# Projection of q, k and v in an attention layer: one float32 product in place of three float32r products, conversions of two blocks at once, stores with longer runs

## The chip, the cores and the metric

One Trainium2 chip, one core of it. The metric is the device time of one launch in microseconds (us). Shorter is better.

## The reference

A transformer layer on x of shape (4, 2048, 256) in float32: normalization, sliding-window attention with 16 heads of 16, and a feed-forward part with ternary weights. The change concerns the first lines, in which q, k and v are made for all 8192 tokens.

```python
xn = _layernorm(x)
q = (xn @ Wq.T).reshape(Bb, Tt, H, HD).transpose(0, 2, 1, 3)
k = (xn @ Wk.T).reshape(Bb, Tt, H, HD).transpose(0, 2, 1, 3)
v = (xn @ Wv.T).reshape(Bb, Tt, H, HD).transpose(0, 2, 1, 3)
logits = jnp.einsum('bhqd,bhkd->bhqk', q, k) * SCALE      # |i-j| <= 128, or token 0
out = jnp.einsum('bhqk,bhkd->bhqd', softmax(where(attend, logits, -inf)), v)
x = x + out.transpose(0, 2, 1, 3).reshape(Bb, Tt, D) @ Wo.T
x = x + bitlinear(relu(bitlinear(_layernorm(x), w_fc) + gate * low_rank)**2, w_proj)
```

## The kernel before, in words

Three stages follow each other: `stage_project` (q, k, v, and the row of token 0), `stage_attend`, `stage_feed`. Only the first is rewritten; in the second only the loads of v follow a new layout in DRAM.

**The loop.** The 8192 tokens are 16 groups of 512 (4 tiles of 128). `step(body, i)` runs a software pipeline on every engine: in iteration i the group i is loaded, i-1 gets its statistics (`n`, LN), i-2 its factor (`f`, LF), i-3 is scaled and transposed (`t`, LT), and i-4 is multiplied (`q`, LP). Order within an engine is the order of the code; between engines there are semaphores only.

**TensorE (PE).** One iteration has four products u = 0..3 (q block 0, q block 1, k block 0, k block 1; each 128 of the 256 outputs by 512 tokens, one PSUM bank each, `qk_bank[u]`), then four products of v (128 tokens by 272 columns, in two banks by turns). `turn()`, the 8 transposes of the next group (L528), stands between u = 2 and u = 3 and waits for `norm.s_scaled`, which ScalarE raises after the last of four scalings (L233). The operands are split: `xt_hi` is the float32r rounding of the transposed x, `xt_lo` the rest, and the weights likewise. `three_pass` makes hi x hi, hi x lo and lo x hi, for two halves of the contraction: six matmuls (L253, L254, L255) for each u and for each v tile. The trace prints float32r operands of matmuls as f32; the names `_hi` and `_lo` tell them apart.

**ScalarE (ACT).** It scales x into `xn` (L233), rounds each finished bank to bf16 (`high`, L608), rounds the rest (`mid`, L613), makes `xt_hi` (L655), and moves v to SBUF (`v`, L618).

**VectorE (DVE).** `rest_of` (L729, L733) subtracts the high part, L761 makes `xt_lo`; the rest is statistics (L142, L202), the factor (`factor_begin`, `factor_end`), and `weights.dve_part`, preparation of the ternary weights.

**GpSimd (POOL).** L448 makes the low bf16 part of q and k, and L459 fills the columns between key blocks (`s_gap`).

**SyncE (SP)** issues every DMA. An iteration: load of x, stores of three parts of q as they are done, three stores of k after `s_gap`, one store of v. After the last group it issues the loads of unit 1, waits for all stores and for the row of token 0 (`s_rv`), stores the row, and only then ends its stage. After the last product the row takes a chain of its own: L573, L576, L581 (64 float32 products of 272 columns, on four column groups of the array), L585 (one float32 product of 272 columns).

Of the kernel before, what the change touches and what calls it, by code (L numbers as in the profile page):

```python
# [31 lines left out]
P = 128  # L32
# [12 lines left out]
VROW = H * VW  # L45
EPS = 1e-5
# [226 lines left out]
def stage_project(nc, x, attn_w, q_dram, k_dram, va_dram, o_dram, weights, sh):  # L273
# [6 lines left out]
    NB, QR, VS = T // P, 32, VROW + VW  # L280
    with ExitStack() as ctx:  # L281
# [10 lines left out]
        xt_hi = sb("xt_hi", [P, 2, KT, GT], F32R)  # L292
        w_in = sb("w_in", [P, 3, KT, D])
        wt_hi = sb("wt_hi", [P, 2, KT, D], F32R)
        wt_lo = sb("wt_lo", [P, 2, KT, D], F32R)
        wv_hi = sb("wv_hi", [P, B, KT, D + H], F32R)
        wv_lo = sb("wv_lo", [P, B, KT, D + H], F32R)
# [9 lines left out]
        xt_lo = sb("xt_lo", [P, 2, KT, GT], F32R)  # L307
# [3 lines left out]
        q_parts = sb("q_parts", [P, 2, KT, PARTS, GT], BF16)  # L311
        k_parts = sb("k_parts", [P, 2, KT, PARTS, KGT], BF16)
        key0, one = sb("key0", [P, KT, PARTS], BF16), sb("one", [P, PARTS], BF16)
# [8 lines left out]
        banks = [ctx.enter_context(nc.psum_tensor(f"p_bank{i}", [P, GT], F32)) for i in range(8)]  # L322
# [10 lines left out]
        s_wt, s_whi, s_wlo, s_wv = sem("w_turned"), sem("w_hi"), sem("w_lo"), sem("wv_copies")  # L333
        s_x0, s_x0v, s_x0sd, s_x0pe = sem("x0_in"), sem("x0_vector"), sem("x0_sd"), sem("x0_tensor")
        s_chi, s_clo = sem("c_hi"), sem("c_lo")
        s_x = [sem(f"x_in{i}") for i in range(4)]
        s_t, s_hi, s_lo = sem("turned"), sem("xt_hi"), sem("xt_lo")
# [16 lines left out]
        def part_of(q, u, part):  # L354
            place = PLACE[u // KT][part]
            if u < KT:
                return q_parts[:, q.par, u, place, :].rearrange("p (n e) -> p n e", e=P)
            return k_parts[:, q.par, u - KT, place, :].rearrange("p (n e) -> p n e", e=KPITCH)[:, :, 1:KPITCH]

        def blocks(bank):  # L360
            return bank[:].rearrange("p (n e) -> p n e", e=P)
# [4 lines left out]
        def _(sp):  # L366
# [15 lines left out]
            def body(at):  # L382
# [8 lines left out]
                if q := at(LP):  # L391
                    rows = q_dram[bass.ds(q.g, 1)].rearrange("a i d s h m t -> (a i d) s (h m t)")
                    for part, done in ((HIGH, s_high), (MID, s_mid), (LOW, s_low)):
                        sp.wait_ge(done, q.g * 4 + KT)
                        sp.dma_start(rows[:, PLACE[0][part]], q_parts[:, q.par, :, PLACE[0][part]]
                                     ).then_inc(s_qout[q.par], DMA)
                    rows = k_dram[bass.ds(q.g, 1)].rearrange("a i d s h m t -> (a i d) s (h m t)")
                    sp.wait_ge(s_gap, q.g * KT + KT)
                    for place in range(PARTS):
                        sp.dma_start(rows[:, place], k_parts[:, q.par, :, place]).then_inc(s_kout[q.par], DMA)  # L400
# [16 lines left out]
        def _(pool):  # L417
# [4 lines left out]
            pool.memset(va[:, :, 0:VROW].rearrange("p n (h e) -> p n h e", e=VW)[:, :, :, HD:VW], 1.0  # L422
# [14 lines left out]
            def wv_copies(b):  # L437

                pool.wait_ge(s_whi, 4)
                pool.tensor_copy(wv_hi[:, b, :, 0:D], wv_hi[:, 0, :, 0:D]).then_inc(s_wv, 1)  # L440
                pool.wait_ge(s_wlo, 3)
                pool.tensor_copy(wv_lo[:, b, :, 0:D], wv_lo[:, 0, :, 0:D]).then_inc(s_wv, 1)

            def body(at):
                if q := at(LP):
                    for u in range(2 * KT):
                        pool.wait_ge(s_mid, q.g * 4 + u + 1)
                        pool.tensor_tensor(part_of(q, u, LOW), rest[:, u, :].rearrange("p (n e) -> p n e", e=P),  # L448
                                           part_of(q, u, MID), ALU.subtract).then_inc(s_low, 1)
                        if u < KT:  # L450
                            continue
                        m = u - KT
                        keys = k_parts[:, q.par, m].rearrange("p s (n e) -> p s n e", e=KPITCH)
                        pool.wait_ge(s_low, q.g * 4 + u + 1)
                        if q.of_batch == 0:
                            wait(pool, s_gap, (q.g - 1) * KT + m + 1)
                            pool.tensor_tensor(key0[:, m, :], keys[:, :, 0, 1], one[:], ALU.mult).then_inc(s_key0, 1)
                            pool.wait_ge(s_key0, q.batch * KT + m + 1)
                        pool.tensor_tensor(keys[:, :, :, 0], key0[:, m, :].unsqueeze(2).broadcast_to([P, PARTS, TB]),  # L459
                                           one[:].unsqueeze(2).broadcast_to([P, PARTS, TB]), ALU.mult  # L460
                                           ).then_inc(s_gap, 1)
# [13 lines left out]
        def _(pe):  # L475
# [13 lines left out]
            def first_queries():  # L489
                pe.wait_ge(s_x0v, 10)  # L490
                pe.wait_ge(s_whi, 2)
# [25 lines left out]
            def wv(tile, q):  # L517
                return [tile[:, bass.ds(q.batch, 1), k, :].rearrange("p a n -> p (a n)") for k in range(KT)]

            def body(at):  # L520
                def turn():

                    if q := at(LT):
                        pe.wait_ge(norm.s_scaled, q.g + 1)
                        for k in range(KT):
                            wait(pe, s_lo, (q.g - 1) * KT + k + 1)
# [1605 lines left out]
```

## Time and profile before

| | us |
|---|---|
| median of three runs (1153.77, 1153.78, 1153.89) | 1153.78 |
| span of the profiled execution | 1152.4 |
| projection products, first to last | 13.2 to 166.7 |
| row of token 0, end of the first stage | 166.7 to 183 |
| attention and feed-forward | 183 to 1152.4 |

The page gives the span of the profiled execution, from first to last instruction, and no other time of it; the span is 1.4 us below the median of the timed runs. Starts in the timeline are us from the beginning of the span. A matmul's row starts when it starts to stream; its end is modelled and includes the pipeline behind it, so rows overlap, and what one costs its successor is the distance of the starts.

### The profile page before, as it was taken

The numbers are of one execution on the slowest core, as the hardware profiler recorded it, in microseconds if no ns is written. First come the engines' busy times: TensorE is split into PE (matmuls) and PEld (weight loads), VectorE is DVE, ScalarE is ACT, GpSimd is POOL, SyncE is SP. The second block draws the span as 40 slices with busy tenths as digits, with TensorE's granted clock in tenths as the row PEclk, the third lists the DMA queues.
The fourth block names the chain that finished last, engine by engine and source line by source line (L and its number), as shares of the span: only waits on it lengthen the run. The fifth ranks groups of instructions, "written<-read, shape, count | busy, mean of one in ns | idle before, by whom it ended". The sixth has DMA issues, their size and how long they took to land.

```text
span 1152.4 us, 26576 instructions
## 1 busy us (share of the span) xinstructions
PE 1126.9 (98%) x9115; PEld 785.0 (68%) x9115; DVE 979.5 (85%) x3169; ACT 843.4 (73%) x1513; POOL 706.8 (61%) x935
## 2 busy tenths in 40 slices
PE   9999997999999999999999999999999999999998
PEld 8888884455555555555555455558888988898887
DVE  7889857899889998899889999867888888888885
ACT  7989983788888888888788888875465546554654
POOL 3665565677778777887778877773344334433443
PEclk9999998999999999999999999999999999999999
DMA  6999897555555555545565554240232113211201
GB/s 199 295 296 281 257 266 168 114 131 118 137 133 122 132 125 136 132 115 137 126 138 130 114 138 108 68 139 29 74 102 64 56 55 102 64 55 56 74 20 37
DMA packets 158166, 145.24 MB, mean 126 GB/s; under 512 B 21564, under 2 KB 157776, under 8 KB 158032
## 3 DMA queue, kind: packets, MB, share of 16 engines
q1 hardware_dynamic: 158032, 143.54, 48.8%
q8 instruction: 73, 1.20, 0.5%
q14 instruction: 61, 0.50, 0.2%
HBM read 91.74 MB, written 50.95 MB: 124 GB/s over the span
## 4 chain that ended last, share of the span: by engine, by line
PE 73%; DVE 7%; issue 2%; ACT 1%; POOL 1%; DVEq 0%; POOLq 0%; ACTq 0%
PE e_psum L1549 15%; PE e_psum L1503 15%; PE e_psum L1527 14%; PE e_psum L1844 6%; PE e_psum L1846 5%; PE e_psum L1267 3%; PE e_psum L1825 3%; PE e_psum L1824 3%; DVE n_stats L142 2%; DVE f_x L1958 2%; PE e_psum L1829 1%; PE e_psum L255 1%; PE e_psum L254 1%; PE e_psum L253 1%; PE e_psum L1793 1%
## 5 line engine op out<-in xcount | busy, mean ns | idle before, releaser
L1665 DVE CUSTOM_DVE_ANT_0 a_masked<-e_psum,band 128x387 f32<-128x387 f32 (+1 forms) x1024 | 493.3, 534 | 58.8 <-PE e_psum L1503 55.8
L1622 ACT ACTIVATE a_weights<-e_psum 128x1024 f32<-128x1024 f32 (+1 forms) x512 | 398.0, 806 | 87.2 <-PE e_psum L1527 82.2
L1401 POOL TENSOR_SCALAR_AFFINE_SELECT a_weights<-a_weights 128x1024 f32<-128x1024 f32 x256 | 276.2, 1091 | 59.9 <-ACT a_weights L1622 58.7
L1503 PE MATMUL e_psum<-e_k,e_q 96*128 96x387 bf16 (+1 forms) x1024 | 281.4, 327 | 3.0 <-PEq L281 1.4
L1888 POOL TENSOR_TENSOR f_square<-f_relu 128x512 f32<-128x512 f32 x128 | 146.1, 1142 | 209.6 <-ACT f_relu L1877 198.6
L1527 PE MATMUL e_psum<-e_q,e_k 128*128 128x384 bf16 (+2 forms) x1408 | 255.6, 279 | 1.5 <-ACT a_weights L1622 1.1
L1549 PE MATMUL e_psum<-a_weights,a_v 128*17 128x384 f32 (+2 forms) x2816 | 195.8, 392 | 1.0 <-POOL a_weights L1401 1.0
L1527 PEld LDWEIGHTS e_psum<-e_q,e_k 128*128 128x128 bf16 x1408 | 129.0, 98 | 95.6 <-issue 39.5
L1503 PEld LDWEIGHTS e_psum<-e_k,e_q 96*128 96x128 bf16 x1024 | 100.4, 98 | 99.2 <-DVE a_max L1665 44.8
L1844 PE MATMUL e_psum<-w_w_t,f_square_hi 128*128 128x256 f32 x512 | 129.4, 287 | 5.6 <-DVE f_square_lo L1934 5.6
L1846 PE MATMUL e_psum<-w_w_t,f_square_lo 128*128 128x256 f32 x512 | 126.8, 282 | 0.0
L1877 ACT ACTIVATE f_relu<-e_psum,w_mag 128x512 f32<-128x512 f32 x128 | 87.2, 681 | 52.6 <-PE e_psum L1829 52.6
L1934 DVE TENSOR_TENSOR f_square_lo<-f_square,f_square_hi 128x512 fp32r<-128x512 f32 x128 | 98.5, 789 | 24.2 <-POOL f_square L1888 24.2
L1549 PEld LDWEIGHTS e_psum<-a_weights,a_v 128*17 128x17 f32 x2816 | 61.7, 96 | 67.5 <-issue 53.6
L1844 PEld LDWEIGHTS e_psum<-w_w_t,f_square_hi 128*128 128x128 f32 x512 | 96.7, 189 | 15.1 <-DVE f_square_lo L1934 12.1
L1824 PE MATMUL e_psum<-f_xt_hi,w_w_t 128*128 128x512 f32 x256 | 102.8, 402 | 1.1 <-ACT f_relu L1877 1.1
L1825 PE MATMUL e_psum<-f_xt_lo,w_w_t 128*128 128x512 f32 x256 | 101.3, 396 | 0.0
L1846 PEld LDWEIGHTS e_psum<-w_w_t,f_square_lo 128*128 128x128 f32 x512 | 97.0, 189 | 2.8
L1880 ACT ACTIVATE f_square_hi<-f_relu 128x512 fp32r<-128x512 f32 x128 | 81.0, 633 | 4.1
L448 POOL TENSOR_TENSOR p_q_parts<-p_rest,p_q_parts 128x512 bf16<-128x512 f32 x32 | 38.3, 1196 | 70.0 <-ACT p_q_parts L613 69.9
L1665 DVE DVE_READ_ACCUMULATOR2_ANT a_max<- 128x1 f32 x1024 | 78.9, 77 | 0.0
L1870 ACT ACTIVATE f_z<-e_psum 128x512 fp32r<-128x512 f32 x16 | 9.6, 597 | 90.1 <-PE e_psum L1816 90.1
(219 smaller groups left out, 2059.0 us busy)
## 6 DMA issues: line engine op xcount, KB each, us to landing
k_parts<-p_k_parts SPq DMA_DIRECT2D x48, 258.0 KB, 4.6
e_k<-k_parts SPq DMA_DIRECT2D x64, 193.5 KB, 3.6
e_k<-k_parts SPq DMA_DIRECT2D x192, 64.5 KB, 3.3
q_parts<-p_q_parts SPq DMA_DIRECT2D x48, 256.0 KB, 5.1
e_q<-q_parts SPq DMA_DIRECT2D x64, 192.0 KB, 3.7
e_q<-q_parts SPq DMA_DIRECT2D x192, 64.0 KB, 3.3
v_ones<-p_va SPq DMA_DIRECT2D x16, 544.0 KB, 5.9
p_x<-in_x SPq DMA_DIRECT2D x16, 512.0 KB, 6.3
```

Source lines behind the costliest of these rows:

```text
L1401: pool.affine_select(out=blocks, in_=blocks, compare_op=ALU.is_ge, fill=0.0, base=0, pattern=[[0, NQ // 2 * HEAD_COLS // P // CUT_STEP], [ ...
L1503: pe.matmul(sh.tile_bank(ux, j)[:, lo:hi], qw[ux.q][0:SLOT_ROWS, h, t * P:t * P + P], kt[ux.hq][0:SLOT_ROWS, h, start + lo:start + hi], st ...
L1527: ins = pe.matmul(score[third // 2][:, c0:c0 + m * P], kt[us.hq][:, h, k0:k0 + P], qw[us.q][:, h, qb * P:(qb + m) * P], start=True, stop=True)
L1549: ins = pe.matmul(sum_bank[32 * j:32 * j + VW, qb * P:(qb + m) * P], vw[:, up.gpar, kb + 1, h * VW:h * VW + VW], pe_w[:, up.upar, c0:c0 + ...
L1622: act.activation(pe_w[:, us.upar, lo:hi], score[c % 2][:], ACT.Exp).then_inc(s_exp, 1)
L1665: dve.tensor_tensor_reduce(out=masked[:, ux.upar, h, t:t + hi - lo], in0=bank[:, lo:hi], in1=band[:, lo:hi], scale=1.0, scalar=NEG, op0=AL ...
L1824: pe.matmul(self.h_bank[j % 2][:], lhs, self.sh.xt_hi[:, q.par, k, :], start=(k == 0), stop=False)
L1825: pe.matmul(self.h_bank[j % 2][:], lhs, self.sh.xt_lo[:, q.par, k, :], start=False, stop=False)
L1844: pe.matmul(y, sh.r2_hi[:, j % 4, part], self.w.w2_t[:, j, :], start=(j == 0 and t == 0), stop=False, skip_group_check=True)
L1846: ins = pe.matmul(y, sh.r2_lo[:, j % 4, part], self.w.w2_t[:, j, :], start=False, stop=(j == MH - 1), skip_group_check=True)
L1888: pool.tensor_tensor(sh.r2[:, j % 4, :], sh.r[:, j % 4, :], sh.r[:, j % 4, :], ALU.mult).then_inc(self.s_sq, 1)
L1934: dve.tensor_tensor(sh.r2_lo[:, j % 4, :], sh.r2[:, j % 4, :], sh.r2_hi[:, j % 4, :].bitcast(F32), ALU.subtract).then_inc(self.s_r2lo, 1)
```

## The change

- `three_pass` goes from q, k and v. Each u and each v tile is two float32 matmuls (the two halves of the contraction), accumulated.
- `xt_lo`, `wt_lo`, `wv_lo` and what made them go. The transposed x (`xt`) is float32: half 0 is copied by ScalarE, half 1 by VectorE, one copy of 512 columns each.
- `high`, `rest`, `mid` and `low` work on two blocks (1024 columns, two PSUM banks) at a time: once for q, once for k. `high(Q)` stands where `high(0)` stood, and waits for u = 0 and u = 1. The scalings of tiles 2 and 3, which stood behind `high(0)` and `high(1)`, both stand behind `high(Q)`.
- `q_parts` and `k_parts` in SBUF have the part outside the block, so that a store moves 2048 or 2064 bytes per partition in one run where it moved two runs of half that. `va_dram` is [128, 64, 289] instead of [8192, 272]: a store or load moves the whole of a partition in one run. `vw` in the second stage is 289 wide. SBUF stays filled with unused pieces (`hole0` to `hole2`) in place of the tensors that went.

```diff
                 if q:
-                    pe.wait_ge(s_lo, q.g * KT + KT)
-                    xh = [xt_hi[:, q.par, k, :] for k in range(KT)]
-                    xl = [xt_lo[:, q.par, k, :] for k in range(KT)]
+                    for k in range(KT):
+                        pe.wait_ge(s_xt[k], q.g + 1)
                 for u in range(2 * KT):
                     if u == KT + 1:
                         turn()
...
-                        wait(pe, s_rest, (q.g - 1) * 4 + u + 1)
-                        three_pass(pe, qk_bank[u][:], [wt_hi[:, w, k, m:m + P] for k in range(KT)],
-                                   [wt_lo[:, w, k, m:m + P] for k in range(KT)], xh, xl).then_inc(s_qk, 1)
+                        if u % KT == 0:
+                            wait(pe, s_rest, (q.g - 1) * 2 + w + 1)
+                        for k in range(KT):
+                            ins = pe.matmul(qk_bank[u][:], wt[:, w, k, m:m + P], xt[:, q.par, k, :],
+                                            start=(k == 0), stop=(k == KT - 1))
+                        ins.then_inc(s_qk, 1)
...
-                        three_pass(pe, v_bank[t % 2][:, 0:D + H], [a[:, cut] for a in xh], [a[:, cut] for a in xl],
-                                   wv(wv_hi, q), wv(wv_lo, q)).then_inc(s_v, 1)
+                        for k in range(KT):
+                            ins = pe.matmul(v_bank[t % 2][:, 0:D + H], xt[:, q.par, k, t * P:(t + 1) * P],
+                                            wv[:, q.batch, k, :], start=(k == 0), stop=(k == KT - 1))
+                        ins.then_inc(s_v, 1)
...
+                def high(w):
+                    act.wait_ge(s_qk, q.g * 4 + w * KT + KT)
+                    wait(act, (s_qout, s_kout)[w][q.par], q.half * DMA * STORES)
+                    act.activation(part_of(q, w, HIGH), products(w), ACT.Copy,
+                                   scale=QSCALE if w == Q else 1.0).then_inc(s_high, 1)
...
                 if q:
-                    high(0)
+                    high(Q)
...
                     norm.scale_act(act, xb[:, t.ring], xn[:, t.par], t, (2,))
-                if q:
-                    high(1)
-                if t and t.g != 1:
                     norm.scale_act(act, xb[:, t.ring], xn[:, t.par], t, (3,))
-                if q:
-                    high(2)
...
-                    sp.dma_start(va_dram[bass.ds(q.g * GT, GT), :].rearrange("(t p) n -> p t n", p=P),
-                                 va[:, bass.ds(q.g * TB, TB), 0:VROW]).then_inc(s_vstored, DMA)
+                    sp.dma_start(va_dram[:, q.g * TB:(q.g + 1) * TB, :], va[:, q.g * TB:(q.g + 1) * TB, :]
+                                 ).then_inc(s_vstored, DMA)
```

On ScalarE, one iteration of the steady part of the projection reads as follows before, from the scaling of tiles 0 and 1 to the first copy of v (`p_bank` are the PSUM banks, `p_rest` the rests):

```order
L233 ACTIVATE p_xn<-p_x,n_shift,n_rstd 128x256 x2
L608 ACTIVATE p_q_parts<-p_bank 128x512
L207 ACTIVATE n_stddev<-n_meanvar,n_eps 128x4
L233 ACTIVATE p_xn<-p_x,n_shift,n_rstd 128x256
L608 ACTIVATE p_q_parts<-p_bank 128x512
L233 ACTIVATE p_xn<-p_x,n_shift,n_rstd 128x256
L608 ACTIVATE p_k_parts<-p_bank 128x4x128
L655 ACTIVATE p_xt_hi<-p_bank 128x512 x2
L613 ACTIVATE p_q_parts<-p_rest 128x512
L608 ACTIVATE p_k_parts<-p_bank 128x4x128
L618 ACTIVATE p_va<-p_bank 128x17x16
```

The same iteration on ScalarE in the changed kernel, to its end (`p_psum` are the PSUM banks as one tensor):

```order
L234 ACTIVATE p_xn<-p_x,n_shift,n_rstd 128x256 x2
L612 ACTIVATE p_q_parts<-p_psum 128x1024
L208 ACTIVATE n_stddev<-n_meanvar,n_eps 128x4
L234 ACTIVATE p_xn<-p_x,n_shift,n_rstd 128x256 x2
L651 ACTIVATE p_xt<-p_psum 128x512
L612 ACTIVATE p_k_parts<-p_psum 128x8x128
L621 ACTIVATE p_va<-p_psum 128x17x16 x2
L617 ACTIVATE p_q_parts<-p_rest 128x1024
L621 ACTIVATE p_va<-p_psum 128x17x16 x2
L617 ACTIVATE p_k_parts<-p_rest 128x8x128
```

The last two scalings stood apart, each behind one block of q; now both stand behind the conversion of the two blocks together.

On TensorE, the changed kernel's iteration, from u = 0 to the first product of the next one (each matmul is one row here, whatever it becomes on the chip; before there were 18, 8, 6, 24 in the same places):

```order
L550 MATMUL p_psum<-p_xt,p_wt 128x512 x6
L530 MATMUL p_psum<-p_ident,p_xn 128x128 x8
L550 MATMUL p_psum<-p_xt,p_wt 128x512 x2
L562 MATMUL p_psum<-p_wv,p_xt 128x272 x8
```

The transposes stay in their place: six products ahead of them, of which only the last two (u = 2) come after what `high(Q)` waits for.

## Rows read from the trace of the kernel before

**Rows 1.** The page: span; engine, busy us, share, instructions.

```profile
span 1152.4 us, 26576 instructions
PE 1126.9 (98%) x9115; PEld 785.0 (68%) x9115; DVE 979.5 (85%) x3169; ACT 843.4 (73%) x1513; POOL 706.8 (61%) x935
```

**Rows 2.** Stretches: us; busy of PE, PEld, DVE, ACT, POOL; granted clock; DMA share; GB/s.

```profile
13.20:166.70 153.50, 152.97 (x896) 133.60 (x897) 127.78 (x331) 137.21 (x298) 86.86 (x111) 1.00 0.93 264
91.39:100.95 9.56, 9.56 (x59) 8.35 (x57) 9.30 (x23) 8.77 (x20) 5.22 (x7) 1.00 0.96 286
```

**Rows 3.** Timeline of PE over one iteration: start, us, engine, line, operation.

```profile
91.39 0.40 PE L253 MATMUL p_bank<-p_xt_hi,p_wt_hi 128*128 128x512 f32 x1
...
94.19 0.40 PE L253 MATMUL p_bank<-p_xt_hi,p_wt_hi 128*128 128x512 f32 x1
...
95.35 0.40 PE L255 MATMUL p_bank<-p_xt_hi,p_wt_lo 128*128 128x512 f32 x1
95.58 1.04 PE L528 MATMUL p_bank<-p_ident,p_xn 128*128 128x128 f32 x8
96.38 0.49 PE L253 MATMUL p_bank<-p_xt_hi,p_wt_hi 128*128 128x512 f32 x1
...
97.87 0.29 PE L253 MATMUL p_bank<-p_wv_hi,p_xt_hi 128*128 128x272 f32 x1
...
100.14 0.35 PE L253 MATMUL p_bank<-p_wv_hi,p_xt_hi 128*128 128x272 f32 x1
...
100.95 0.40 PE L253 MATMUL p_bank<-p_xt_hi,p_wt_hi 128*128 128x512 f32 x1
```

**Rows 4.** Timeline of PE behind the projection: float32 products with four column groups, then one.

```profile
169.95 2.50 PE L487 MATMUL p_bank<-p_ones 128*128 128x128 f32 x20
172.62 7.53 PE L581 MATMUL p_bank<-p_va,p_w 128*16 128x272 f32 x128 [0.16 <-ACT p_w L681]
181.04 0.62 PE L585 MATMUL p_bank<-p_picked,p_seq_of 128*4 128x272 f32 x2 [0.90 <-DVE p_picked L819]
```

**Rows 5.** Line L585: duration ns min/median/max, first and last start.

```profile
L585 PE MATMUL p_bank<-p_picked,p_seq_of x2: 393/393/393, 181.0 to 181.3; 128*4 128x272 f32 x2
```

**Rows 6.** Timeline of ACT around the transposes of the iteration of rows 3.

```profile
93.48 0.29 ACT L207 ACTIVATE n_stddev<-n_meanvar,n_eps 128x4 f32<-128x4 f32 x1
93.67 0.59 ACT L233 ACTIVATE p_xn<-p_x,n_shift,n_rstd 128x256 f32<-128x256 f32 x1
94.38 0.60 ACT L608 ACTIVATE p_q_parts<-p_bank 128x512 bf16<-128x512 f32 x1
94.88 0.59 ACT L233 ACTIVATE p_xn<-p_x,n_shift,n_rstd 128x256 f32<-128x256 f32 x1
```

**Rows 7.** An ACT read of 1024 columns of PSUM, 183 to 290 us; count, busy, mean ns.

```profile
L1622 ACT ACTIVATE a_weights<-e_psum 128x1024 f32<-128x1024 f32 x39 | 39.9, 1024 | 10.7 <-PE e_psum L1527 9.9
```

**Rows 8.** Timeline of PE and PEld ahead of the first product of the projection.

```profile
10.53 0.86 PEld L528 LDWEIGHTS p_bank<-p_ident,p_xn 128*128 128x128 f32 x8 [0.65 <-ACT p_xn L233]
12.28 0.64 PE L480 MATMUL p_bank<-p_ident,p_w_in 128*128 128x128 f32 x4
13.21 0.50 PE L253 MATMUL p_bank<-p_xt_hi,p_wt_hi 128*128 128x512 f32 x1 [0.29 <-DVE p_xt_lo L761]
```

**Rows 9.** Groups within 13.2 to 166.7 us; count, busy us, mean ns, idle before.

```profile
L448 POOL TENSOR_TENSOR p_q_parts<-p_rest,p_q_parts 128x512 bf16<-128x512 f32 x32 | 38.3, 1196 | 70.0 <-ACT p_q_parts L613 69.9
L729 DVE SCALAR_TENSOR_TENSOR p_rest<-p_bank,p_q_parts 128x512 f32<-128x512 f32 x32 | 22.0, 688 | 15.3 <-ACT p_q_parts L608 15.0
L613 ACT ACTIVATE p_k_parts<-p_rest 128x512 bf16<-128x512 f32 x32 | 20.3, 635 | 1.2 <-DVE p_rest L733 1.2
L618 ACT ACTIVATE p_va<-p_bank 128x272 f32<-128x272 f32 x63 | 25.1, 399 | 2.6 <-PE p_bank L255 2.1
```

**Rows 10.** Timelines of SP, POOL and DVE in the tail of the first stage.

```profile
170.07 2.28 SPq L400 DMA_DIRECT2D k_parts<-p_k_parts  x3
180.24 1.53 SPq L1230 DMA_DIRECT2D e_q<-q_parts  x3
182.21 0.26 SPq L414 DMA_DIRECT2D attention<-row  x1
169.57 0.25 POOL L459 TENSOR_TENSOR p_k_parts<-p_key,p_one 128x12 bf16<-128x12 bf16 x1
181.70 0.41 DVE L823 COPY row<-p_bank 4x256 f32<-4x256 f32 x1 [0.71 <-PE p_bank L585]
```

More of the change, by code:

```diff
@@ L45 @@
 VROW = H * VW
+VS = VROW + VW
 EPS = 1e-5
@@ L321, in stage_project @@
         row, s_row = sh.row, sh.s_row0
-        banks = [ctx.enter_context(nc.psum_tensor(f"p_bank{i}", [P, GT], F32)) for i in range(8)]
+        psum = ctx.enter_context(nc.psum_tensor("p_psum", [P, 8, GT], F32))
+        banks = [psum[:, i, :] for i in range(8)]
         t_bank, qk_bank, v_bank = banks[0:2], banks[2:6], banks[6:8]
@@ L352, in stage_project, with part_of, products, rest_of @@
         LN, LF, LT, LP = 1, 2, 3, 4
[L354 to L361, printed above, removed]
+        Q, K = 0, 1
+        def part_of(q, w, part):
+            place = PLACE[w][part]
+            if w == Q:
+                return q_parts[:, q.par, place].rearrange("p m (n e) -> p (m n) e", e=P)
+            return k_parts[:, q.par, place].rearrange("p m (n e) -> p (m n) e", e=KPITCH)[:, :, 1:KPITCH]
+        def products(w):
+            return psum[:, 2 + KT * w:2 + KT * w + KT, :].rearrange("p m (n e) -> p (m n) e", e=P)
+        def rest_of(w):
+            return rest[:, KT * w:KT * w + KT, :].rearrange("p m (n e) -> p (m n) e", e=P)
         block = ctx.enter_context(nc.Block())
@@ L437, in wv_copies @@
             def wv_copies(b):
[L439 to L442, printed above, removed]
+                pool.wait_ge(s_wc, 4)
+                pool.tensor_copy(wv[:, b, :, 0:D], wv[:, 0, :, 0:D]).then_inc(s_wv, 1)
             def body(at):
                 if q := at(LP):
[L446 to L461, printed above, removed]
@@ new lines, in body @@
+                    for w in (Q, K):
+                        pool.wait_ge(s_mid, q.g * 2 + w + 1)
+                        pool.tensor_tensor(part_of(q, w, LOW), rest_of(w), part_of(q, w, MID), ALU.subtract
+                                           ).then_inc(s_low, 1)
+                    keys = k_parts[:, q.par].rearrange("p s m (n e) -> p s m n e", e=KPITCH)
+                    pool.wait_ge(s_low, q.g * 2 + 2)
+                    if q.of_batch == 0:
+                        wait(pool, s_gap, q.g)
+                        pool.tensor_tensor(key0[:], keys[:, :, :, 0, 1], one[:].unsqueeze(2).broadcast_to([P, PARTS, KT]),
+                                           ALU.mult).then_inc(s_key0, 1)
+                        pool.wait_ge(s_key0, q.batch + 1)
@@ L462, in body @@
+                    for m in range(KT):
+                        ins = pool.tensor_tensor(keys[:, :, m, :, 0], key0[:, :, m].unsqueeze(2).broadcast_to([P, PARTS, TB]),
+                                                 one[:].unsqueeze(2).broadcast_to([P, PARTS, TB]), ALU.mult)
+                    ins.then_inc(s_gap, 1)
                     if 1 <= q.g < B:
```

164 lines of the change are left out of this document (63 added, 101 removed).

## The prediction

> **What bounds the kernel now.** I read the page first: TensorE is busy for 98% of the span, VectorE for 85% [rows 1]. Such an average says nothing of one stage, so I cut the projection out, and one iteration of it. In the 153.5 us from the first to the last product TensorE is idle for 0.5 us; in the iteration from 91.39 to 100.95 it is never idle, while VectorE has 9.30 of 9.56 us busy, ScalarE 8.77, GpSimd 5.22, and the DMA engines 0.96 [rows 2]. TensorE sets the pace of this stage, the others follow with little room. The clock granted is 1.00, the full 2.4 GHz [rows 2]. What the edit does to TensorE therefore shows in full, and what it does for the other engines and the stores shows only if TensorE has to wait for them.
>
> **The distance of starts on TensorE, before.** u = 0 to 2 are 18 float32r matmuls of 512 columns in 95.58 - 91.39 = 4.19 us, 0.2328 each. The transposes take 96.38 - 95.58 = 0.80 us, and u = 3, six matmuls, 97.87 - 96.38 = 1.49 us, which is 0.09 over six times 0.2328, for the weights that are loaded in the open behind the transposes. So transposes cost 0.89. v: the first 18 matmuls take 100.14 - 97.87 = 2.27 us, 0.126 each; all 24 take 3.08, with a short hitch in front of the last tile [rows 3]. Sum: 24 x 0.2328 + 0.89 + 3.08 = 9.56, the iteration.
>
> **What a float32 product costs.** The rows have float32 products too, with real operands: L585 is one matmul in the code and two rows on the chip, of 393 ns each, and the two together last 0.62 us; so the second starts 0.62 - 0.393 = 0.227 us behind the first [rows 4, 5]. One float32 product of 272 columns thus takes two instructions of 0.227 us, 0.454 in all, where three float32r ones take 3 x 0.126 = 0.378. L581 says the same in bulk: 128 instructions for 64 products, 7.53 us, with four column groups at work at a time; (7.53 - 0.39)/127 x 4 = 0.225 [rows 4]. 0.227 us for 272 columns is 0.834 ns a column, twice what one pass at 2.4 GHz needs; two instructions make four passes.
>
> L581 and L585 load narrow weights. The rows with 128 x 128 float32 weights are L487: 20 instructions of 128 columns in 2.50 us, (2.50 - 0.27)/19 = 0.117 [rows 4], against 0.107 by columns; so up to 0.010 an instruction is to be added, and I take half. For 512 columns no float32 row exists: 512 x 0.834 = 0.427 is the floor, twice 0.2328 = 0.466 the ceiling, if a float32 pass streams no faster than a float32r one. I take 0.433, near the floor, since at 272 columns the float32 instruction (0.227) is clearly below twice the float32r one (0.252). For v I take 0.232, between 0.227 and 0.252.
>
> - q and k: 16 instructions x 0.433 = 6.93 us, where 24 x 0.2328 = 5.59 were: +1.34.
> - v: 16 x 0.232 = 3.71, where 3.08 were: +0.63.
> - Together +1.97 an iteration, 16 iterations: **+31.5 us.**
>
> The Trainium skill ("FP8 and Floating Point Precision", TensorE Precision Notes) says that a true float32 product takes four passes through the array; L585 agrees with its 0.454 us, four passes of 0.113 us. The rule alone would price a pass by the float32r rows; that result is rival B below.
>
> **A wait that the new order makes.** `turn()` waits for the last scaling. Now this is queued on ScalarE behind `high(Q)`, which waits for u = 1. Let T be the time when u = 1 has streamed. Before, its last matmul ended streaming at 94.19 and its conversion began at 94.38: 0.19 [rows 3, 6]. The conversion of 1024 columns out of PSUM: L1622 has 1.02 us [rows 7], and ScalarE starts the next instruction 0.1 before the end of the last (0.60 long, next after 0.50) [rows 6], so 0.92. The root of the variance 93.48 to 93.67: 0.19. The scaling of tile 2: 0.50, of tile 3 to its end: 0.59 [rows 6]. From there to the first transpose 0.06 (the end of a scaling at about 10.48, its weight load at 10.53 [rows 8]). T + 0.19 + 0.92 + 0.19 + 0.50 + 0.59 + 0.06 = T + 2.45. TensorE is there after u = 2: T + 4 x 0.433 = T + 1.73. It waits 0.72 us. Before, the same chain had only half a conversion behind u = 1 and was over at 95.47, just before 95.58 [rows 3, 6], so the wait is new. It occurs where both a group to multiply and a group to transpose are there, without the first (group 1 is scaled early): 14 times, **+10.1 us**. Queued behind TensorE's wait are u = 3 and v, all of the rest.
>
> **Does another wait appear?** With an iteration of 6.93 + 0.89 + 0.72 + 3.71 = 12.25 us, I followed each engine through it, S being the end of u = 3. ScalarE: `high(K)` begins at S + 0.19, the first copy of v ends at S + 1.5 (0.40 long [rows 9]); the third v tile needs it at S + 1.86. The next scalings start at about S + 5.2 and end at S + 6.3, ahead of the next T at S + 7.2. VectorE loses one of the two 512-column passes behind the transposes and keeps about 9 us of 12.25; its passes over 1024 columns are below twice 0.69 us [rows 9] and each bank has over 3 us before it is written again. GpSimd's are below twice 1.2 us [rows 9] and make 5.2 of 12.25. The stores have half the runs and a longer iteration. All of these edits, the fused conversions (a saving of about 0.1 us each), the missing `xt_lo`, the longer runs, I cost at nothing: behind TensorE's 12.25 us. If TensorE were not the bound, they would be worth something, see the third rival. The loads of v in the attention stage are prefetched; nothing waits for them in the rows, so nothing is gained.
>
> **Ends.** The first product waited 0.29 us for `xt_lo`, which is gone [rows 8]: **-0.3**. In the tail, SP was busy with its issues until 180.24 + 1.53 = 181.77, and the row was ready at 182.11 [rows 10], so only 0.3 us lay between. SP's chain begins when the last key columns are filled: 169.57 + 0.25 = 169.82, 3.10 us after the last product (166.72). Now ScalarE's `mid(K)` (0.96) stands behind the last copy of v, and GpSimd's `low(K)` of two blocks (2.3) and two fills behind that: mid(K) ends 1.5 us after the last product, low(Q) keeps GpSimd until 2.0, low(K) until 4.3, the fills until 4.9. That is 1.8 later, less the 0.3 to 0.4 of room and less what shorter stores save in issue, which I can't read: between 0 and 1.5, I take **+1.1** (the row's own chain moves with the products).
>
> **Sum** against the profiled execution: 1152.4 + 31.5 + 10.1 - 0.3 + 1.1 = 1194.8 us; the runs shown lie 1.4 above their span, which gives 1196.2 us.
>
> **The rivals.**
> - *B, slower still: a float32 pass streams at the float32r distance.* For it: float32r at 512 columns takes 0.2328, not 0.213, and I have no float32 row of that width with wide weights. Against it: L585. Then 16 x 0.466 = 7.45 and 16 x 0.252 = 4.03: +2.81 an iteration, 45.0; the wait shrinks to 2.45 - 1.86 = 0.59, 8.3; with the ends 54.1: 1207.9 us. By the rule of four passes from the page named above and the float32r row, this would be the time. Chance 0.12.
> - *C, the products at their floor and no wait at the transposes* (if ScalarE converts two banks faster, or the release of the bank is earlier than I think). 16 x 0.427 + 16 x 0.227 = 10.46, against 8.67: +1.79, 28.6, with the ends 29.4: 1183.2 us. With half of the wait it is some 1188. Chance 0.14.
> - *D, faster: one float32 instruction costs no more than one float32r instruction*, so that two take the place of three. This needs 0.2328 at 512 columns, and decides for a gain as soon as an instruction is below 0.33 or so. Then TensorE needs 3.72 + 0.89 + 2.02 = 6.6, and waits 2.45 - 0.93 = 1.5 at the transposes: 8.15; VectorE and ScalarE with some 8.4 us would be the bound: 16 x (8.4 - 9.56) = -18.6: 1136 us. For it: only that the distance of L487 may be set by its weight load. Against it: L585, where nothing but streaming lies between the two starts, and L581. Chance 0.03.
> - *E, the edit moves TensorE little in either direction*, because something else than the columns sets the distances: within 0.2% of before, chance 0.01.
> - The forecast, with waits a little longer or shorter: 1188 to 1204 us, chance 0.70.
>
> **How the numbers follow.** The likeliest is 1196.2. Below 1183 I leave D, E and part of C, 0.08; above 1209 what lies beyond B (a chain that comes late on VectorE or SP as well), 0.08. Two thousandths of the time, 2.3 us, is about what a measurement of this kernel can tell from no change. Faster by more than that: D alone, 0.03. No change: E, 0.01. Slower: the rest, 0.96.
>
> **What the profile after would show.** Right: L550 with twice its count of instructions (256 rows), starts 0.43 apart; L562 0.23 apart; an iteration of 12.2 to 12.3 us; PE idle in front of L530 with ScalarE's L234 as releaser, some 0.7 us, 14 times; VectorE and ScalarE with 3 us idle in each iteration; the attention stage as long as before. Wrong: starts of L550 at 0.47 (B), at 0.23 (D), no idle time before L530 (C), or PE waiting for `p_rest`, `p_xt` or `p_va`.

## The result and the profile after

The changed kernel takes 1196.26 us (median of three runs, 1194.24 to 1196.48), the kernel before 1153.78; the ratio is 1.036, 95% interval 1.034 to 1.038. Slower, as forecast, and close to the 1196.2 of the prediction. Whether its terms are right is another matter, and one of them isn't.

The page of the changed kernel, its head:

```profile
span 1194.2 us, 25872 instructions
PE 1160.0 (97%) x8859; PEld 761.7 (64%) x8859; DVE 973.0 (81%) x3115; ACT 831.8 (70%) x1433; POOL 696.2 (58%) x896
PEclk9999999889999999999999999999999999999999
```

Three stretches of it, columns as in [rows 2]: the products of the projection, the row of token 0, the rest.

```profile
12.77:206.07 193.30, 185.63 (x642) 109.55 (x641) 121.36 (x278) 125.55 (x218) 75.12 (x73) 1.00 0.67 219
206.07:224.89 18.82, 14.83 (x170) 9.68 (x169) 12.17 (x28) 5.14 (x7) 11.08 (x14) 0.91 0.67 168
224.89:1194.20 969.31, 948.38 (x7976) 632.01 (x7976) 831.97 (x2773) 694.31 (x1195) 605.06 (x793) 0.99 0.41 101
```

The same stretches of the kernel before:

```profile
13.21:166.72 153.51, 152.99 (x897) 133.62 (x898) 127.77 (x331) 137.22 (x298) 86.88 (x111) 1.00 0.93 264
166.72:183.07 16.35, 13.28 (x171) 8.17 (x170) 10.83 (x28) 4.71 (x7) 9.66 (x15) 1.00 1.04 263
183.07:1152.40 969.33, 949.39 (x7976) 632.93 (x7976) 832.06 (x2773) 694.15 (x1195) 605.37 (x793) 0.99 0.41 100
```

The first product starts 0.44 us earlier, the products take 39.8 us more, the row 2.5 more, and attention with feed-forward is the same to 0.02 in these two profiles (over all thirteen profiles of this document it lies between 968.0 and 970.0 us, so a difference of a microsecond there says nothing). Together 41.8 us, the difference of the spans. The medians differ by 42.5: the time outside the span is 2.1 us here (1196.26 with a span of 1194.2) and was 1.4. TensorE is idle for 7.7 of its 193.3 us, where it was 0.5 (all of that 0.5 in one iteration, which took 10.47 us where the others took 9.5 to 9.6: the scaling came late there, by 0.52 us, as the row below shows); VectorE is busy for 63% of the stretch where it was 83%, the DMA engines 0.67 for 0.93.

```profile
76.47 1.09 PE L528 MATMUL p_bank<-p_ident,p_xn 128*128 128x128 f32 x8 [0.52 <-ACT p_xn L233]
```

One iteration on TensorE, the answer to [rows 3]. The rows are merged where nothing lies between the instructions:

```profile
98.22 5.31 PE L550 MATMUL p_psum<-p_xt,p_wt 128*128 128x512 f32 x12
104.09 1.09 PE L530 MATMUL p_psum<-p_ident,p_xn 128*128 128x128 f32 x8 [0.56 <-ACT p_xn L234]
105.02 1.88 PE L550 MATMUL p_psum<-p_xt,p_wt 128*128 128x512 f32 x4
106.74 3.83 PE L562 MATMUL p_psum<-p_wv,p_xt 128*128 128x272 f32 x16
110.41 5.31 PE L550 MATMUL p_psum<-p_xt,p_wt 128*128 128x512 f32 x12
```

Six matmuls in the code are 12 instructions, as L585 foretold. One lasts 0.592 (median of L550), so their distance is (5.31 - 0.592)/11 = 0.429 us; u = 3 takes (106.74 - 105.02)/4 = 0.43; v takes (110.41 - 106.74)/16 = 0.229. The iteration is 12.19 us. In front of the transposes the profile names ScalarE's scaling. From the end of streaming (98.22 + 12 x 0.429 = 103.37) to 104.09 it is 0.72 us; the 0.56 of the row is less because the modelled end of the last product reaches past its streaming.

ScalarE in this stretch, the answer to [rows 6]:

```profile
101.85 1.02 ACT L612 ACTIVATE p_q_parts<-p_psum 128x1024 bf16<-128x1024 f32 x1 [1.11 <-PE p_psum L550]
102.77 0.29 ACT L208 ACTIVATE n_stddev<-n_meanvar,n_eps 128x4 f32<-128x4 f32 x1
102.96 1.08 ACT L234 ACTIVATE p_xn<-p_x,n_shift,n_rstd 128x256 f32<-128x256 f32 x2
104.84 0.60 ACT L651 ACTIVATE p_xt<-p_psum 128x512 f32<-128x512 f32 x1 [0.81 <-PE p_psum L530]
```

This is the chain of the prediction: ScalarE had waited 1.11 us for u = 1, then converts 1024 columns, takes the root, scales two tiles until 104.04, and the transposes start at 104.09. While it does so TensorE comes to rest (a rest is, here and below, time in which it streams nothing).

The tail is what follows the last product: a chain of small steps in turn on TensorE and VectorE makes the row of token 0. `m_diag`, a diagonal of maxima that VectorE writes, is one link of it. First what TensorE does there:

```profile
207.64 0.27 PE L578 MATMUL p_psum<-p_ident,p_m_tok 128*64 128x128 f32 x1
210.12 0.43 PE L581 MATMUL p_psum<-p_m_diag,p_ones 64*128 64x64 f32 x2 [1.77 <-DVE p_m_diag L776]
210.48 4.10 PE L492 MATMUL p_psum<-p_ones 128*128 128x128 f32 x20
```

Here are two losses the forecast didn't have: 1.77 us idle for `m_diag`, where it was 0.60, and 4.10 us for the 20 products that took 2.50 [rows 4]. VectorE and GpSimd at that place:

```profile
207.96 2.06 POOL L454 TENSOR_TENSOR p_k_parts<-p_rest,p_k_parts 128x1024 bf16<-128x1024 f32 x1
208.27 1.80 DVE L776 TENSOR_SCALAR p_m_diag<-p_ident,p_m_neg 64x64 f32<-64x64 f32 x1
```

GpSimd's instruction ends at 210.02, VectorE's at 210.07. In the kernel before the two end at 169.49 and 169.54:

```profile
168.37 1.12 POOL L448 TENSOR_TENSOR p_k_parts<-p_rest,p_k_parts 128x512 bf16<-128x512 f32 x1
168.91 0.63 DVE L806 TENSOR_SCALAR p_m_diag<-p_ident,p_m_neg 64x64 f32<-64x64 f32 x1
```

And the granted clock around it, in the changed kernel:

```profile
209.00:210.10 1.10, 0.00 (x0) 0.00 (x0) 1.07 (x1) 1.08 (x2) 1.02 (x2) 1.00 0.62 238
210.10:212.00 1.90, 1.88 (x11) 1.81 (x12) 1.41 (x6) 0.28 (x1) 1.69 (x6) 0.76 0.15 58
212.00:214.50 2.50, 2.50 (x13) 2.29 (x11) 2.36 (x9) 1.06 (x1) 2.50 (x3) 0.50 1.03 395
214.50:218.00 3.50, 3.50 (x65) 1.79 (x68) 3.08 (x8) 0.00 (x0) 2.90 (x4) 1.00 0.99 221
```

Behind the idle time the clock is at 0.50, the 1.2 GHz level, and at 1.00 again from 214.5. It doesn't fall in the rest itself: it is 1.00 until 211.0, when TensorE has been at work again for 0.9 us, and falls in the half microsecond after:

```profile
211.00:211.50 0.50, 0.50 (x5) 0.50 (x5) 0.50 (x3) 0.00 (x0) 0.50 (x2) 0.60 0.00 0
```

Before, it was 1.00 all through 166.7 to 183.

### The profile page after: what moved, and what is told of

Same layout as the page of the kernel before. It is cut to its first block, busy times and chain, and to the rows that moved or that the text cites. A ratio compares the mean times of both kernels' runs of the same rounds, so it can differ in the third digit from the quotient of the medians.

```text
span 1194.2 us, 25872 instructions
## 1 busy us (share of the span) xinstructions
PE 1160.0 (97%) x8859; PEld 761.7 (64%) x8859; DVE 973.0 (81%) x3115; ACT 831.8 (70%) x1433; POOL 696.2 (58%) x896
## 3 DMA queue, kind: packets, MB, share of 16 engines
q8 instruction: 71, 1.16, 0.4%
## 4 chain that ended last, share of the span: by engine, by line
PE 70%; DVE 7%; issue 2%; ACT 1%; POOL 0%; DVEq 0%; POOLq 0%; ACTq 0%
PE e_psum L1518 15%; PE e_psum L1472 14%; PE e_psum L1496 14%; PE e_psum L1813 5%; PE e_psum L1815 5%; PE e_psum L1237 3%; PE e_psum L1794 3%; PE e_psum L1793 3%; DVE n_stats L143 2%; DVE f_x L1927 2%; PE e_psum L1798 1%; PE e_psum L256 1%; PE e_psum L255 1%; PE e_psum L254 1%; PE e_psum L1762 1%
## 5 line engine op out<-in xcount | busy, mean ns | idle before, releaser
L1634 DVE CUSTOM_DVE_ANT_0 a_masked<-e_psum,band 128x387 f32<-128x387 f32 (+1 forms) x1024 | 493.4, 534 | 58.6 <-PE e_psum L1472 55.6
L550 PE MATMUL p_psum<-p_xt,p_wt 128*128 128x512 f32 x256 | 115.2, 593 | 0.0
L454 POOL TENSOR_TENSOR p_q_parts<-p_rest,p_q_parts 128x1024 bf16<-128x1024 f32 x16 | 34.2, 2136 | 122.9 <-ACT p_q_parts L617 122.9
```

Of the source, the lines that this page charges most:

```text
L550: ins = pe.matmul(qk_bank[u][:], wt[:, w, k, m:m + P], xt[:, q.par, k, :], start=(k == 0), stop=(k == KT - 1))
L1634: dve.tensor_tensor_reduce(out=masked[:, ux.upar, h, t:t + hi - lo], in0=bank[:, lo:hi], in1=band[:, lo:hi], scale=1.0, scalar=NEG, op0=AL ...
```

## The experiments

Each time stands beside the kernel before on the same chip, whose median was 1153.13 in the first four, 1153.42 in the second four, 1152.51 for the ninth and tenth and 1152.69 for the last. Single runs of before spread over 1151.4 to 1155.4, so a difference of 1 us between kernels of different sets is none. Two repairs come up again and again: "the scalings ahead" takes away the wait at the transposes, "the halves" shortens the wait for `m_diag`.

### The products alone (on the kernel before)

```diff
-                        three_pass(pe, qk_bank[u][:], [wt_hi[:, w, k, m:m + P] for k in range(KT)],
-                                   [wt_lo[:, w, k, m:m + P] for k in range(KT)], xh, xl).then_inc(s_qk, 1)
+                        for k in range(KT):
+                            ins = pe.matmul(qk_bank[u][:], wt_hi[:, w, k, m:m + P], xh[k], start=(k == 0), stop=(k == KT - 1))
+                        ins.then_inc(s_qk, 1)
```

and the same for v; the `_hi` tensors are float32.

> The kernel before with the products alone changed: two float32 matmuls instead of six float32r ones; the low parts are still computed, by the same instructions, and nothing reads them. Theory (the columns price the products): q and k 16 x 0.429, v 16 x 0.229, transposes 0.93, so 11.46 us an iteration against 9.56, 16 x 1.90 = 30.4, no wait at the transposes since only half a conversion and one scaling stand behind u = 1 (T + 1.34 against T + 1.72): 1184 us. Rival (the loss comes from the fused conversions and what waits for them, not from the products): under 1165 us.

Measured: 1181.32 us, ratio 1.024 (1.023 to 1.026). The timeline of TensorE, one iteration:

```profile
106.23 5.31 PE L548 MATMUL p_bank<-p_xt_hi,p_wt_hi 128*128 128x512 f32 x12
111.38 1.04 PE L528 MATMUL p_bank<-p_ident,p_xn 128*128 128x128 f32 x8
112.25 1.88 PE L548 MATMUL p_bank<-p_xt_hi,p_wt_hi 128*128 128x512 f32 x4
113.97 3.83 PE L560 MATMUL p_bank<-p_wv_hi,p_xt_hi 128*128 128x272 f32 x16
117.64 2.74 PE L548 MATMUL p_bank<-p_xt_hi,p_wt_hi 128*128 128x512 f32 x6
```

No wait at the transposes, 11.41 us. The products cost 11.41 - 9.56 = 1.85 us an iteration, 29.6 in all. The estimate was 2.7 us high. The kernel before has 0.65 us less in this set; the transposes take 0.87 when they follow products without a rest, not the 0.93 of the changed kernel, which is 0.8 in all; and this kernel's own tail is 0.4 us shorter than before. The remaining 0.8 us is no more than what attention and feed-forward differ by between profiles (968.2 here, 969.3 before). The rival that puts the loss on the conversions falls.

### The other parts, with float32r products

The changed kernel with `three_pass`, the low parts and their subtractions back; fused conversions, long runs and the order on ScalarE stay.

> The changed kernel with the three float32r products back (hi and lo parts made as before), fused conversions and long runs kept. Theory: the wait at the transposes is a matter of the order on ScalarE: T + 2.45 against T + 6 x 0.2328 = T + 1.40, so 1.05 us, 14 times, 14.7 us, and the tail as long as in the changed kernel, +2.5: 1171 us. Rival (fused conversions and long runs pay once the float32 products no longer cover them; VectorE, ScalarE and the DMA engines were near their limit before): 1154 us or less.

Measured: 1171.89 us, ratio 1.016 (1.014 to 1.018). The timeline of TensorE, the transposes of two iterations:

```profile
115.26 1.09 PE L532 MATMUL p_psum<-p_ident,p_xn 128*128 128x128 f32 x8 [0.89 <-ACT p_xn L234]
126.01 1.09 PE L532 MATMUL p_psum<-p_ident,p_xn 128*128 128x128 f32 x8 [0.88 <-ACT p_xn L234]
```

10.75 us from one to the next. The estimate was 1171, and the rival (1154 or less) falls. The wait is larger where the products are shorter, since ScalarE's chain is the same: a price that doesn't come with float32, and that no fused conversion pays back.

### The scalings ahead of the conversion of q

```diff
-                if q:
-                    high(Q)
-                if f and f.g != 1:
-                    norm.root_eps(act, f)
                 if t and t.g != 1:
                     norm.scale_act(act, xb[:, t.ring], xn[:, t.par], t, (2,))
                     norm.scale_act(act, xb[:, t.ring], xn[:, t.par], t, (3,))
+                if q:
+                    high(Q)
+                if f and f.g != 1:
+                    norm.root_eps(act, f)
```

> The changed kernel with the scalings of tiles 2 and 3 ahead of the conversion of the two blocks of q, nothing else. Theory: the 0.72 us in front of the first transpose go, 14 times, 10.1 us, and the conversion starts some 0.3 us late, which nobody waits for: 1186 us. Rival (the wait moves on to the next semaphore, to the rests of q or the copies of x): 1193 us or more.

Measured: 1184.2 us, ratio 1.027 (1.025 to 1.028). The timeline of TensorE, one iteration:

```profile
104.97 5.31 PE L550 MATMUL p_psum<-p_xt,p_wt 128*128 128x512 f32 x12
110.12 1.04 PE L530 MATMUL p_psum<-p_ident,p_xn 128*128 128x128 f32 x8
110.99 1.88 PE L550 MATMUL p_psum<-p_xt,p_wt 128*128 128x512 f32 x4
112.71 3.83 PE L562 MATMUL p_psum<-p_wv,p_xt 128*128 128x272 f32 x16
116.38 4.03 PE L550 MATMUL p_psum<-p_xt,p_wt 128*128 128x512 f32 x9
```

The wait is gone and the iteration 11.41 us, that of the products alone. So a wait costs 12.19 - 11.41 = 0.78 us (0.72 of rest and 0.06 of transposes that start from rest). Thirteen of the 14 cost that and the last 0.59, together 10.7 us: the products, first to last, take 182.6 us here and 193.3 in the changed kernel. The rival falls: the wait doesn't move on. In this profile TensorE was idle in the tail for 1.77 us as well, and yet the 20 products took 2.50, so the tail is 1.4 us shorter; that is most of what the estimate missed, and not a merit of this edit.

### The new layouts alone (on the kernel before)

```diff
-        q_parts = sb("q_parts", [P, 2, KT, PARTS, GT], BF16)
-        k_parts = sb("k_parts", [P, 2, KT, PARTS, KGT], BF16)
+        q_parts = sb("q_parts", [P, 2, PARTS, KT, GT], BF16)
+        k_parts = sb("k_parts", [P, 2, PARTS, KT, KGT], BF16)
...
-    va_dram = nc.dram_tensor("v_ones", [N, VROW], F32, kind="Internal").ap()
+    va_dram = nc.dram_tensor("v_ones", [P, N // P, VS], F32, kind="Internal").ap()
```

> The kernel before with the new layouts alone: parts outside the block in SBUF, v in DRAM as one run per partition; conversions and products as before. Theory: the DMA engines are at 0.96 before but set nothing, so the same within 0.2%: 1153.8 us, DMA share in the projection clearly lower. Rival (the stores hold up x or the key chain): 1150 us or less.

Measured: 1151.76 us (ten runs), ratio 0.9985 (0.9976 to 0.9995): faster by 0.15%, so not quite nothing, though less than the 0.2% named as the bound. The DMA share of the projection is 0.82 for 0.93. In the profile the products take 152.6 us for 153.5, TensorE idle for 0.01 us of it where it was 0.5. The profile before has VectorE waiting for the DMA of x, 2.5 us in two waits, the longer 2.1 us at 64.7 to 66.8 (its view of waits); this one has a single such wait, of 0.3 us. The one iteration of before that took 10.47 us comes from that long wait: VectorE was late with its rests, ScalarE waited 1.16 us for one of them (until 72.39) and was late with the scalings, and TensorE with the transposes at 76.47. Here no iteration is over 9.6. So what the shorter stores took away in the projection is one late load of x: the rival was right in kind, once in 16 groups. That the load was late because of the stores is likely, but one pair of profiles doesn't show it. What is left of the 1.4 us is of the size by which attention and feed-forward differ between profiles (968.0 here, 969.3 before).

### The tail: GpSimd's low parts of the last group in halves

```diff
-                        pool.tensor_tensor(part_of(q, w, LOW), rest_of(w), part_of(q, w, MID), ALU.subtract
-                                           ).then_inc(s_low, 1)
+                        n = KT * TB
+                        for c in ([slice(0, n // 2), slice(n // 2, n)] if q.g == G - 1 else [slice(0, n)]):
+                            ins = pool.tensor_tensor(part_of(q, w, LOW)[:, c], rest_of(w)[:, c],
+                                                     part_of(q, w, MID)[:, c], ALU.subtract)
+                        ins.then_inc(s_low, 1)
```

> The changed kernel with GpSimd's low parts of the last group in two instructions each. Theory: VectorE's step of the row's chain (the diagonal of maxima, 1.80 us where it was 0.63) ends when the GpSimd instruction beside it ends; with halves it ends 1.0 us sooner, TensorE stands idle 0.7 us and not 1.8, and if the idle time is what lets the granted clock fall, another 1.4 us go: 1194 to 1195 us for the wait alone, 1193.8 with the clock. Rival (the step is slow for its own reasons): 1196.3 us, the step still 1.8 us.

Measured: 1193.47 us, ratio 1.035 (1.0335 to 1.0363). The timeline of VectorE:

```profile
208.27 0.99 DVE L779 TENSOR_SCALAR p_m_diag<-p_ident,p_m_neg 64x64 f32<-64x64 f32 x1
```

VectorE's step is 0.81 us shorter and TensorE's rest 0.96 us; the 20 products behind take 2.50 us:

```profile
209.68 2.50 PE L495 MATMUL p_psum<-p_ones 128*128 128x128 f32 x20
```

The profile's span is 1191.2 us, 3.0 below the changed kernel's: 0.8 of the wait, 1.4 of the clock, and 0.9 behind the row, in attention and feed-forward (968.4 for 969.3 us), which no edit touched.

### The tail: products in the gap

```diff
             pe.wait_ge(s_rv, 3)
```

is preceded by `idle_products(total_bank, 6)`, work that nothing reads.

> The changed kernel with six idle products of 128 columns (1.4 us) in TensorE's gap of the row's chain, ahead of the wait for the diagonal. Theory: the wait stays, 1.8 us, but the granted clock of the stretch behind stays at 1.00 and the 20 instructions behind take 2.5 us and not 4.1: 1194.8 us. Rival (the clock falls for another reason): 1196.3 us.

Measured: 1194.85 us, ratio 1.036 (1.034 to 1.037). `m_diag` still takes 1.79 us, and TensorE comes to it at 210.10, as in the changed kernel; but its rest is 0.42 us, and behind it:

```profile
210.46 2.50 PE L492 MATMUL p_psum<-p_ones 128*128 128x128 f32 x20
```

The rows settle it, not the time: the four runs lie in two pairs, 1193.9 and 1194.1, 1195.6 and 1195.8, and those of the changed kernel at 1194.2 and at 1196.3 and 1196.5.

So the wait and the clock are two things, and the second follows the idle time. Over all profiles, that of the kernel before among them: with a rest of at most 1.21 us at this place (nine of them) the 20 products take 2.50 us; with 1.77 to 2.0 us they take 4.05 to 4.13 in three and 2.50 in one, that of the scalings ahead. A long rest lets the clock fall, but not each time.

### Both repairs

The scalings ahead and the halves in the last group.

> The changed kernel with both repairs: scalings ahead of the conversion of q, and the low parts of the last group in halves. Theory: both add up, -10.1 and -1 to -2.5: 1183.7 to 1185 us, all that is left over before being the products. Rival (the two share a cause): 1186 us or more.

Measured: 1182.93 us, ratio 1.026 (1.024 to 1.027). The two add up, and nearly all that is left is the price of the products. It is 1.6 us above the products alone (1181.32), and the runs of the two don't overlap (1182.4 to 1184.2, 1180.6 to 1182.4): TensorE's rest for `m_diag` is still 0.97 us where the products alone have 0.22, and the time outside the span is 2.1 us where it is 1.7.

### Float32r products with the scalings ahead

> Float32r products, fused conversions and long runs, and the scalings ahead of the conversion of q. Theory: no wait at the transposes, TensorE's own sum of 9.5 us an iteration, the tail of the changed kernel (+2.5) less 0.4 to 1: 1155 us, no gain over before, since TensorE bounds both. Rival (the freed time of the others is worth something): under 1150 us.

Measured: 1158.48 us, ratio 1.004 (1.003 to 1.006). The wait at the transposes is gone, but an iteration is 9.6 to 9.9 us, not 9.5, and the tail has 2.0 us of rest and the slow clock. The estimate was 3.5 us low; the rival (under 1150) falls.

### The same with the halves in the last group

> Float32r products, fused conversions and long runs, scalings ahead of the conversion of q, and the low parts of the last group in halves. Theory: the tail's 1 us of wait and, if the clock stays, another 1.5 us go from the 1158.5 of the run without halves: 1156 us, still no gain over before; the fused conversions and long runs are worth nothing under a TensorE bound. Rival (they are worth something once both waits are gone): under 1152 us.

Measured: 1155.81 us, ratio 1.003 (1.002 to 1.004). The estimate was 1156. The tail is repaired (1.20 us of rest, the 20 products in 2.50), and the kernel still behind before. In 57 us of its projection VectorE is busy for 55.6 (stretch, busy time of PE, PEld, DVE, ACT, POOL, clock, DMA):

```profile
91.00:148.00 57.00, 56.94 (x328) 48.80 (x326) 55.58 (x121) 49.65 (x89) 29.12 (x26) 1.00 0.78 264
```

### Halves in every group, in the changed kernel

The condition on the last group is gone from the diff above.

> The changed kernel with GpSimd's low parts in halves in every group. Theory (VectorE's operations that read SBUF alone stand still until the GpSimd instruction beside them ends): the ternary step that takes 1.8 us on average in the projection of the changed kernel comes back to 1.1 or less, the time stays where the kernel with halves in the last group alone is, 1193.5 us, since VectorE is not the bound. Rival (GpSimd and VectorE slow each other by what they move, however it is cut): the step stays at 1.8 us.

Measured: 1194.14 us, ratio 1.036 (1.034 to 1.038), as with the last group alone. The ternary step on VectorE, in the changed kernel and in this one (count, busy us, mean ns):

```profile
L999 DVE SCALAR_TENSOR_TENSOR z_w_in<-z_w_in,z_half,z_below 128x256 f32<-128x256 f32 x11 | 19.9, 1805 | 0.4
```

```profile
L1002 DVE SCALAR_TENSOR_TENSOR z_w_in<-z_w_in,z_half,z_below 128x256 f32<-128x256 f32 x11 | 12.1, 1098 | 0.4
```

With GpSimd idle the same step takes 0.48 us (behind 218 us in the changed kernel), and 0.49 beside a GpSimd memset (215.0 us). Beside a subtraction, how long it takes is set by the length of that instruction, not by what GpSimd does in all. The theory holds for this step, but is too broad as it was put: in the changed kernel a statistics step, which reads SBUF alone too, takes its usual 0.40 us at 88.76, in the middle of a GpSimd subtraction of 2.25 us (87.97 to 90.22). The Trainium skill ("SBUF — State Buffer", "SBUF: two separate sides") says that VectorE in some modes, or with two inputs from SBUF where GpSimd reads SBUF too, shares a pair of ports with GpSimd under an exclusive lock, held for a whole instruction. The traces agree: `m_diag` ends 0.05 us behind GpSimd's instruction (210.02 and 210.07; 169.49 and 169.54), and half as long a GpSimd instruction takes 0.7 us off the mean of the ternary step, which has two inputs from SBUF.

### Float32r products, both repairs, halves in every group

> As the last float32r kernel (fused conversions, long runs, scalings ahead of the conversion of q), but with GpSimd's low parts in halves in every group. In the profiles of its forerunners VectorE was the engine without room (55.6 of 57 us busy) and an iteration took 9.65 to 9.70 us where the kernel with the new layout alone took 9.54. Theory: VectorE is held there by the long GpSimd instructions; with halves an iteration is 9.55 us again, 16 x 0.13 = 2 us less: 1153.8 us beside the 1155.8 of the kernel with halves in the last group alone. Rival (the longer iteration comes from the longer ScalarE or VectorE passes themselves): 1155.8 us, iterations still 9.65.

Measured: 1155.03 us (eleven runs), ratio 1.0025 (1.0016 to 1.0034). VectorE's load falls as expected (52.3 us of the same 57), but an iteration is still 9.62 to 9.74 us in that stretch, and the first instruction behind the products starts at 167.76 us where it was 168.07. VectorE was worth 0.3 us, not 2: the theory fails, and the rival, the longer passes themselves, is nearer. What remains shows on TensorE, and a longer pass of ScalarE stands behind it. Its timeline in front of the third tile of v:

```profile
108.83 0.29 PE L256 MATMUL p_psum<-p_wv_hi,p_xt_lo 128*128 128x272 f32 x1
109.02 0.39 PE L254 MATMUL p_psum<-p_wv_hi,p_xt_hi 128*128 128x272 f32 x1
109.25 0.29 PE L255 MATMUL p_psum<-p_wv_lo,p_xt_hi 128*128 128x272 f32 x1
```

and that of ScalarE, same kernel:

```profile
107.66 1.02 ACT L616 ACTIVATE p_k_parts<-p_psum 128x1024 bf16<-128x1024 f32 x1 [0.68 <-PE p_psum L256]
108.58 0.39 ACT L625 ACTIVATE p_va<-p_psum 128x272 f32<-128x272 f32 x1
```

The third tile needs the bank of the first, whose copy stands behind the conversion of both k blocks and ends at 108.97; it starts at 109.02, and the start before it and its own first distance are 0.19 and 0.23 where the others are 0.125: 0.17 us an iteration (before, with one block converted ahead of the copy, 0.06, in front of the fourth tile [rows 3]). The longer iterations, up to 9.74, have 0.1 us more in front of the transposes. No run moved the copy ahead of the conversion of k, so that the third tile is the cause is read from these rows and not tested. With float32 products the third tile comes 1.83 us after u = 3 and the copy ends at 1.51, early enough. None of the four float32r versions with fused conversions beats before.

## Why the prediction was right, and where it wasn't

- **The bound.** TensorE set the pace before and sets it after. VectorE and ScalarE have 4.5 and 4.2 us of room in each iteration now, and it is worth nothing, as the run with the halves in every group shows: VectorE's ternary steps 7.8 us shorter in all, no time gained.
- **The products.** Predicted 0.433 and 0.232 an instruction, +31.5 us; measured 0.429 and 0.229, and +29.6 us (the products alone, and the scalings ahead, both 11.41 us an iteration). The step from one float32 matmul of 272 columns to 512 columns held; the price lies near the floor (0.427 and 0.227), below the values that I took between floor and ceiling. The transposes, 0.87 for 0.89, did the rest. Rival B (0.466) and rival D (0.233) are out. Rival B priced a float32 pass like a float32r one; but at 512 columns the float32r pass has 0.2328 and the float32 one 0.2145, so four for three cost 1.23 times as much and not 4/3.
- **The wait at the transposes.** Predicted 0.72 us, 14 times, 10.1 us; measured 0.72 of rest, 0.78 with the slower start, 0.59 in the last, 10.7 us in all. Rival C, that it isn't there, is out. Undone by the order alone, as the scalings ahead show.
- **The tail.** Predicted +1.1 us because SP would be late; measured +2.5, and not by SP. This step failed. The chain on SP was over at 218.57 + 1.53 = 220.10, as the timelines of SP and VectorE in the changed kernel show:

```profile
218.57 1.53 SPq L1200 DMA_DIRECT2D e_q<-q_parts  x3
224.11 0.26 SPq L422 DMA_DIRECT2D attention<-row  x1
223.60 0.41 DVE L793 COPY row<-p_psum 4x256 f32<-4x256 f32 x1 [0.71 <-PE p_psum L590]
```

  and waited 4 us for the row, because its issues take less time than before (k 1.82 for 2.28 us, the first load of q 0.54 for 1.60) and the row came later. "The row's own chain moves with the products" is the sentence that was wrong: VectorE's step waits for a GpSimd instruction that had become twice as long (+1.18), and TensorE's clock fell behind the rest that this made (+1.36 up to L586). The halves shorten the step and the rest (0.99 for 1.80, 0.96 for 1.77 us); the idle products leave the step as it is and keep the clock. The first part is shown; that a long rest brings the slow clock is shown for three profiles of four.
- **The start.** -0.3 predicted, -0.44 measured.
- **The edits costed at nothing.** In the steady iteration of this kernel they are nothing: 11.41 us with them and without. In the tail the fused conversions are not, as said. Around float32r products the long runs are worth 0.15%, and the fused conversions, run only together with the long runs, cost: by the wait, by the third tile of v and by the longer GpSimd instructions.
- **The sum.** 31.5 + 10.1 - 0.3 + 1.1 = 42.4 us predicted, 41.8 measured by spans, 42.5 by medians. By the terms it is 29.6 + 10.7 - 0.4 + 2.5 = 42.4; the one late iteration of before (0.9 us) is in none of them, and about 0.3 us is left over. That the total is met to a tenth is luck: the products were 1.9 too high, the wait 0.6 and the tail 1.4 too low, and the 0.7 us by which the time outside the span grew made up for what the spans had less.

Open: why the same rest of 1.77 us was followed by the slow clock in one kernel and not in another; why the time outside the span is longer by 0.4 to 0.7 us in the float32 versions with fused conversions; and whether fused conversions would pay with the copy of v ahead of the conversion of k, or with q alone fused, which no run tried. The three timed runs of the changed kernel have 1196.3, 1196.5 and 1194.2 us, the last with a mean clock of 0.997 for 0.994. That this is the tail's clock isn't shown: with the idle products, whose profile has the tail at full clock, the runs lie in two groups 1.6 us apart as well, and that profile itself belongs to the slower one, with a mean clock of 0.994.

## What to carry to other kernels

Before products are traded for fewer and costlier ones, find one of the costlier kind anywhere in the trace: a single one with two rows showed here that it is two instructions of two passes, and gave the price at 272 columns to 1%, and at 512 as well. When conversions are fused, list what stands behind each on its engine, and who waits for that: two scalings of 0.5 us behind a conversion that began later and took twice as long cost 10.7 us, and moving them ahead gave it back. A longer GpSimd instruction can hold up a VectorE step beside it until it ends; here this befell `m_diag` and the ternary step, and not the statistics. Cut it in two where such a step stands in a chain that TensorE waits for; where nobody waits, as in the other groups here, it gains nothing.

## What the runs showed of the hardware that I had not expected

- VectorE's 64 x 64 step takes 0.25 us with no GpSimd subtraction beside it (the kernel with the products alone has this row), 0.63 to 2.02 with one, always until that ends:

```profile
198.82 0.25 DVE L809 TENSOR_SCALAR p_m_diag<-p_ident,p_m_neg 64x64 f32<-64x64 f32 x1
```

- A float32r matmul of 512 columns starts 0.2328 us before the next, 0.455 ns a column; a float32 one is two instructions of 0.429 us, and if each makes two passes, 0.419 ns a column and pass. The pass in float32 is then the faster one.
- Transposes that start from rest take 0.93 us to the next product, those behind a product 0.87.
